# Reordering the per-tile slot of the local-attention layers: attention's value product behind the projection of v, the output product behind the next projection of q, DVE's maxima ahead of its rotation of k

## What is computed

```python
for i in range(DEPTH):                       # 6 layers
    x = attn_layer(shift_tokens(x), Wqkv[i], q_scale[i], k_scale[i], Wo[i]) + x
    x = ffn_layer(shift_tokens(x), ln_g[i], ln_b[i], W1[i], b1[i], W2[i], b2[i]) + x
```

## Time and profile before

| what | value |
|---|---|
| median of three runs | 3675.78 us (3674.07 to 3676.65) |
| the profiled execution's own time | 3676.79 us |
| its span, first to last instruction | 3675.0 us |
| granted TensorE clock, mean | 0.988 of full speed |
| PE busy | 3518.1 us (96%) |
| DVE busy | 3185.6 us (87%) |
| ACT busy | 2870.5 us (78%) |
| POOL busy | 2576.6 us (70%) |

### The profile page before, as it was taken

How to read it: one execution, slowest core, us unless ns; L and a number is a source line. 1 busy time by engine, 2 the same in 40 slices (tenths; PEclk the granted TensorE clock), 3 DMA queues, 4 the chain that set the end, 5 groups by cost and what they waited for, 6 DMA issues and landing times.

```text
span 3675.0 us, 161687 instructions
## 1 busy us (share of the span) xinstructions
PE 3518.1 (96%) x70540; PEld 2666.8 (73%) x70540; DVE 3185.6 (87%) x4422; ACT 2870.5 (78%) x5288; POOL 2576.6 (70%) x2106
## 2 busy tenths in 40 slices
PE   6999999869999999999999999999999999999996
PEld 2222222358888888888888888888888888888885
DVE  7999999578888988888888889888888888888884
ACT  3999999857777787877777787878777777777774
POOL 3222111278888888888888888888888888888883
PEclk8999999989999999999999999999999999999999
DMA  4110000034444444444444444444444444444432
GB/s 121 40 42 22 23 20 19 16 96 111 122 115 110 126 116 117 117 113 114 128 115 120 113 115 127 113 118 114 114 122 120 117 118 111 132 119 111 115 111 73
DMA packets 210250, 366.48 MB, mean 100 GB/s; under 512 B 37106, under 2 KB 81734, under 8 KB 209222
## 3 DMA queue, kind: packets, MB, share of 16 engines
q1 hardware_dynamic: 209482, 355.05, 35.1%
HBM read 236.73 MB, written 111.67 MB: 95 GB/s over the span
## 4 chain that ended last, share of the span: by engine, by line
PE 46%; DVE 14%; ACT 9%; issue 5%; POOL 5%; ACTq 0%; POOLq 0%; DVEq 0%
PE PB L1447 8%; PE PA L1371 8%; PE PD L1399 6%; PE PD L1460 5%; PE PB L1371 4%; PE PC L1421 4%; PE PC L1499 3%; DVE T L1756 3%; PE PA L1430 3%; PE PC L1475 2%; POOL T L1283 2%; DVE T L1746 2%; DVE T L1750 2%; DVE ss L1762 2%; ACT Vs L1565 1%
## 5 line engine op out<-in xcount | busy, mean ns | idle before, releaser
L1265 POOL TENSOR_TENSOR T<-T 128x1024 f32<-128x1024 f32 x384 | 907.3, 2379 | 8.7 <-DVE T L1756 8.7
L1283 POOL TENSOR_TENSOR T<-T,rn 128x1024 f32<-128x1024 f32 x384 | 731.4, 1905 | 27.7 <-POOL rn L1276 1.3
L1371 PE MATMUL PA<-Wqkv,XS 128*128 128x512 f32 x2304 | 633.0, 410 | 9.8 <-DVE XS L1710 9.1
L759 DVE TENSOR_REDUCE negmax<-p_max 128x1 f32<-128x1024 f32 x512 | 588.9, 1214 | 15.5 <-PE p_max L659 13.4
L821 ACT ACTIVATE E<-p_low 128x512 f32<-128x512 f32 x1024 | 554.0, 596 | 27.7 <-PE p_low L683 16.9
L1371 PEld LDWEIGHTS PA<-Wqkv,XS 128*128 128x128 f32 x2304 | 417.0, 194 | 80.7 <-DVE XS L1710 10.7
L1728 DVE TENSOR_REDUCE sm<-Ew 128x16 f32<-128x1024 f32 x192 | 233.6, 1217 | 236.7 <-ACT Ew L1589 236.7
L1762 DVE TENSOR_REDUCE ss<-SQ 128x32 f32<-128x2048 f32 x192 | 436.9, 2276 | 0.0
L1399 PE MATMUL PD<-ident,T 128*128 128x128 f32 x3072 | 410.7, 277 | 17.5 <-POOL T L1283 16.2
L1447 PEld LDWEIGHTS PB<-ET,VW 64*64 64x64 f32 x24576 | 376.4, 135 | 45.6 <-DVE T L1756 29.6
L1447 PE MATMUL PB<-ET,VW 64*64 64x32 f32 x24576 | 398.2, 220 | 10.6 <-DVE T L1756 5.2
(11 more groups left out here) (167 smaller groups left out, 6988.7 us busy)
## 6 DMA issues: line engine op xcount, KB each, us to landing
VW<-v_rows SPq DMA_DIRECT2D x768, 256.0 KB, 4.6
v_rows<-Vs SPq DMA_DIRECT2D x192, 512.0 KB, 3.4
Wraw<-in_Wqkv SPq DMA_DIRECT2D x40, 192.0 KB, 5.0
QA<-parts_q SPq DMA_DIRECT2D x384, 16.0 KB
KA<-parts_k SPq DMA_DIRECT2D x192, 32.0 KB
fs<-XC SPq DMA_DIRECT2D x48, 127.0 KB
parts_q<-AO SPq DMA_DIRECT2D x8, 384.0 KB, 2.6
parts_k<-AO SPq DMA_DIRECT2D x8, 384.0 KB, 3.3
```

The costliest lines, as they stand in the source:

```text
L759: dve.tensor_reduce(negmax[:, qh, c, qt:qt + 1], p_max[:, k % 2, :], axis=AX.X, op=ALU.max, negate=True).then_inc(s_mr.sem, 1)
L1265: pool.tensor_tensor(out=t_, in0=t_, in1=T2[:, i * HALF:(i + 1) * HALF], op=ALU.add).then_inc(ad.sem, 1)
L1283: pool.tensor_tensor(out=t_, in0=t_, in1=rn[:, p, i * LH:(i + 1) * LH].unsqueeze(2).broadcast_to([P, LH, LD]), op=ALU.mult).then_inc(no.se ...
L1371: mm = pe.matmul(pair[:, half, :], XS[:, b, i, 1:P + 1], Wqkv[:, l % 2, j, lo:lo + 512], start=(k == 0), stop=(k == 2))
```

## The change

On PE, `project_qk(s,0)` goes ahead of `output(s-4)`, and `attend(s-3)` goes behind `input_T(s+1)` and `project_v(s)`. The alignment directive moves from the head of q's projection to the head of `output`, with other offsets. On ACT, v's copy and the exponentials go ahead of the copy of attention's result; the roots come behind it. On DVE, `output` goes behind q's rotation, and the maxima go between q's and k's rotation. On SP, v's way out waits for `output(s-4)` in place of the scores, and its way in for the first copy of q in place of the copy of k.

```diff
 on_sp
-            if is_tile(s - 2):
-                sp.wait_ge(sc.sem, sc.at(s - 2))
+            if is_tile(s - 4):
+                sp.wait_ge(wo.sem, wo.at(s - 4))
             if is_tile(s - 1):
                 values_out(s - 1)
-                sp.wait_ge(te.sem, te.at(s - 1, 3))
+                sp.wait_ge(te.sem, te.at(s - 1, 1))
 on_pe
-    BLOCK, FIRST_Q = 256, (105, 105, 98, 98)
+    BLOCK, FIRST_OUT = 256, (51, 51, 44, 44)
...
-                pe.addr_align(BLOCK, offset=FIRST_Q[b], max_nops=0)      # in project_qk
+            pe.addr_align(BLOCK, offset=FIRST_OUT[b], max_nops=0)        # head of output
...
+            if is_tile(s):
+                project_qk(s, 0)
             if is_tile(s - 4):
                 output(s - 4)
-            if is_tile(s):
-                project_qk(s, 0)
...
                 transpose_qk(s - 1, 1)
-            if is_tile(s - 3):
-                attend(s - 3)
             if is_tile(s + 1):
                 input_T(s + 1)
             if is_tile(s):
                 project_v(s)
+            if is_tile(s - 3):
+                attend(s - 3)
 on_act
+            if is_tile(s):
+                project_v(s)
+            if is_tile(s - 2):
+                exponentials(s - 2)
             if is_tile(s - 3):
                 attend(s - 3)
             if is_tile(s):
-                project_v(s)
                 roots(s)
             if d == 0 and is_step(u - 2):
                 ff_norm(u - 2)
-            if is_tile(s - 2):
-                exponentials(s - 2)
-            if d == 0 and is_step(u - 2):
                 ff_high(u - 2)
 on_dve
+            if is_tile(s):
+                rotate(s, 0)
             if is_tile(s - 4):
                 output(s - 4)
             if d == 3 and is_step(u - 1):
                 ff_rows(u - 1)
             if d == 3 and is_step(u - 2):
                 ff_value(u - 2, 2)
-            if is_tile(s):
-                rotate(s, 0)
-                rotate(s, 1)
             if is_tile(s - 2):
                 maxima(s - 2)
+            if is_tile(s):
+                rotate(s, 1)
```

## The result

The changed kernel takes **4025.24 us** (median of 4 runs, 4017.88 to 4029.43) where the kernel before took 3675.59 us beside it: 1.0949 times the time, with an interval of 1.0931 to 1.0968. That is 350 us slower. The forecast of 3960 us had the direction, but the range ended at 4005 us, 20 us short.

The account below looks back on a forecast made before the run. PE was taken as the bound, with hardly a gap (0.19 us idle in a 14.81 us slot). The terms +276 - 53 + 21 + 38 = +282 us on 3676.8 us gave 3960 us, range 3890 to 4005.

Parts of the forecast that it names:

- Term 1: PE ahead of input_T: it waits for ACT's copies of k out of PD, +1.47 us a slot, +276 us.
- Term 2: PE's present waits and output's weight-load idle mostly go: -0.28 us a slot, -53 us, between 0 and -60.
- Term 3: POOL's loop from attend to k's next transposes holds PE: +0.45 us once a step, +21 us, bounds 0 and 0.7.
- Term 4: Slots d=3: the scores wait for DVE's value 2, +0.8 us once a step, +38 us, bounds 0 and 1.0.
- SP's waits: SP's new waits only start v's transfers earlier; both cost nothing, with cover of some 4 us each.
- Instruction blocks: PE's stalls at boundaries between instruction blocks: 0 to 0.4 us a step, 0 to 19 us, taken as 0.
- the jump waits for its block: The branch over the padding, between q and output, stalls 0.4 us in each slot: 4035 us; chance 0.07.
- the te wait alone: Only PE's wait for ACT's copies and the give-back act; the POOL and value 2 costs vanish: 3900 us; chance 0.15.
- DVE's k rotation gates attend: DVE starts the maxima over 0.9 us late, so attend waits; typical price 0.3 us, 4015 us; chance 0.06.
- No te wait: input_T has no wait for ACT's copies, so the order only gives back: 3624 us; chance 0.04.

Follow-up runs that it names:

- x6: The changed kernel with DVE's order of the kernel before (output first, maxima after k's rotation): 3951.79 us, ratio 1.0752.
- x7: The changed kernel with input_T and project_v exchanged on PE and DVE's order of the kernel before: 3854.72 us, ratio 1.0486.
- x5: The changed kernel with DVE's copy of rows to XC done as a maximum over an axis of one element: 3987.52 us, ratio 1.0855.
- x10: The changed kernel with both of SP's waits as in the kernel before (scores, third count of te): 4264.06 us, ratio 1.1605.
- x13: The changed kernel with only v's way in waiting as before, for the copy of k: 4260.92 us, ratio 1.1586.
- x16: The kernel before with SP's two new waits alone: 3715.21 us, ratio 1.0119.
- x4: The kernel before with DVE's new order alone, PE, ACT and SP as before: 4411.66 us in one run.
- x1: The changed kernel with project_v ahead of input_T on PE: 3941.45 us, ratio 1.0726.
- x2: The changed kernel with PD's bank released after the copy to kT, and kH copied from kT instead of PD: 4080.46 us, ratio 1.1104.

## Why the prediction was right in its direction and wrong in its size

- **Term 1, the wait on te (+276): right.** Its row is the first of PE's waits, 1.39 us in nearly every slot, and the transposes to input_T are 2.43 us (2.44 predicted). As charged it was slightly large: I took 0.97 us for the old distance from one slot, and the mean is 1.03, so 1.40 a slot, 263 us. x6, which keeps all of the change but DVE's new order, lies 275 us above before.
- **Term 2, the give-back (-53): failed, and it is the largest miss.** Only the idle part came, and little of it, 0.05 us a slot. The other 0.09 were taken off output's weight loads, but PE's busy time rose by 0.14 us a slot (27 us) instead. So a term of -53 us measured +18. The chain shows one place: the gates now follow attend and take 1.59 us instead of 1.39. The starts in the timeline show another: from v's first product to the next group are 1.56 us ahead of attend, where they were 1.47 ahead of the gates (medians). Attend's weight loads stand idle 62.0 us in 167 places, against 37.0 in 165 before. The step that failed: the prediction looked at what each group waits for and not at which group it stands behind. That this is the whole of the 27 us is argued from those rows and not shown by a run.
- **Term 3, POOL's loop (+21): nil.** PE waits for T 9 times, 6.9 us in all. PE's path from attend over ff_norm's transposes to k's next ones takes 10.84 us in the median, of which 0.24 are idle in the mean, where I had walked 10.4 for it and 10.8 for POOL: PE is about as long as the loop by itself. x7 shows that the loop is near: with te and DVE's order gone, it costs 27.9 us.
- **Term 4, value 2 on DVE (+38, bounds 0 and 1.0 us): the mechanism right, the size wrong.** PE waits 1.50 us in the mean (61.6/41). Over the 42 steps of the stretch that is 1.47 a step, against 0.02 before (0.7 us in all), so 47 x 1.45 = 68 us, above the upper bound of 1.0; x6 measures DVE's order at 73. The walk had "the rows' copy" at 0.2 us, as an instruction takes that nothing disturbs. It took 1.22, since the new order starts it while POOL multiplies the weights. x5 measures that share alone: 38 us. Without it the wait is 0.76 us, nearly the 0.8 predicted. The Trainium skill ("SBUF — State Buffer", Who interferes with whom) says that a DVE copy can enter a mode that takes the port pair shared with GpSimd for the whole instruction, so that whichever starts second blocks, and that a `tensor_reduce` never contends on trn2. Rows and runs agree: 294 ns undisturbed, 1222 ns with the end 0.16 us behind POOL's, 420 ns always for the reduction.
- **SP's waits ("both cost nothing; their cover is some 4 us each"): the number right, the reason wrong.** As edits of the changed kernel they cost nothing that shows, but not because they are slack. The old ones would have cost 239 us (x10), nearly all by the way in (x13). Put into the old order the new ones cost 40 (x16). I counted what waits for these transfers and left out what else they can hold up: PE stalled by when they ran.
- **Instruction blocks (0, bounds 0 and 19) and the rival "the jump waits for its block" (4035, 0.07).** The number is near 4025, but the mechanism did not act here: ahead of output there are 3.6 us of such waits in 168 slots. It is real all the same, and stronger than the 0.4 us that I had priced: 181.5/118 = 1.5 us a time in x10, up to 2.8. The Trainium skill ("Runtime: NRT & Kernel Launch", Instruction fetch mechanics) says that crossing a boundary is mostly hidden, and that a taken branch to a page not held costs a stall. Here the first is true of the changed kernel, and the second would fit x10 and x13, where v's transfers run just before; that the fetch is what waits is inferred from what moves it, since no row names it.
- **The rival "the te wait alone" (3900)** falls, as x6 and x5 show term 4 in the time. **"DVE's k rotation gates attend"** falls for the change as it stands: attend has no such wait. It is x4's main loss and 26.9 us of x1's. **"No te wait"** falls by the first row of waits.

As sums: predicted 276 - 53 + 21 + 38 = 282 us; found 263 - 9 + 27 + 70 = 351 us. Of the missing 69 us, give-back and busy time are +71, term 4 +32, terms 1 and 3 -34. The range left its upper end at 4005 because it took the upper bounds of term 3, term 4 and the blocks, but not that of term 2, which its own text put at 0: with it the end would have been some 53 us higher. The end would have held if only one of terms 2 and 4 had been off; so the result lies outside through both, and mostly through term 2.

## What to carry to other kernels

When an order puts a group directly behind the one that filled its PSUM bank, the copies out of the bank turn into idle time of TensorE in every round; the slots in which the pipeline fills show that price before the change is built. Of an engine walked, ask of each copy and scaling on DVE what POOL runs at that moment, and check the walk against the start times of both. And a wait that seems only to start a transfer earlier is to be costed against all that uses the DMA engines, and PE's instructions seem to be among it: here moving one such wait is worth 236 us.

## What was not expected of the hardware

- A DVE copy of 128x256 float32 took 294 ns alone and 1222 ns (up to 1771) when it started while a POOL instruction ran. Four small scalings took 1.19 us, and 2.58 where they started 0.17 us behind a POOL product; for them no run tried another instruction. The same data moved by a reduction took 420 ns in all 48 places.
- With v's four transfers (256 KB each) started 1.99 us ahead of attend, output, the first group behind the branch, began late without a releaser in 118 places of 2600 us, 181.5 us in all and up to 2.8 at a time; started 4.57 us ahead, it did so in 8 of 168 slots, 3.6 us in all.
- A wait of 2.01 us on PE was followed by some 3.4 us at the lower clock level (0.50 granted), one of 1.57 us by none. So a wait can cost more than its own length, as x2 shows. The length alone does not decide: a clock below 1.00 followed 33 of x2's 35 waits of about 2.0 us, but 13 of 35 of about 2.3 us in x1 and 12 of 33 of 2.0 to 2.8 us in x10.
- The gates' six products took 1.39 us behind v's projection and 1.59 to 1.60 behind attend, whose tile shape is another, with no wait of theirs or of their weight loads in the rows.
